# Turning the next group's rows between two projections, in the stage between two attentions

## The reference

```
x = x + _layernorm(_L1_attn_ref(...))            # end of the first attention
x = x + _layernorm(_L1_ffn_ref(_layernorm(x), ...))
# inside _L1_ffn_ref, e_cnt = 4, n = t // 4 tokens in each slice e:
for e in range(e_cnt):
    xn = _layernorm(x[:, e * n:(e + 1) * n, :], norm_w, norm_b)
    m = d // 2 ** e                              # 256, 128, 64, 32 features
    xm = xn[..., :m]
    qs.append(jnp.einsum('bnm,dm->bnd', xm, q_w[:, :m]) + q_b)
    ks_.append(jnp.einsum('bnm,dm->bnd', xm, k_w[:, :m]) + k_b)
    vs.append(jnp.einsum('bnm,dm->bnd', xm, v_w[:, :m]) + v_b)
```

## Time and profile before

| | us |
|---|---|
| median of 3 runs | 5305.97 |
| the 3 runs | 5304.77, 5305.97, 5321.23 |
| the profiled execution's own time | 5311.03 |
| its span (first to last instruction) | 5309.0 |
| mean granted TensorE clock in it | 0.927 of full |

### The profile page before, as it was taken

One profiled execution on the slowest core, in us unless ns is written; L12 is line 12 of the kernel. 1 busy time (PEld: TensorE's weight loads), 2 busy tenths in 40 slices (PEclk: granted clock), 3 DMA queues, 4 the chain that ended last, 5 costly groups with the idle time before them and its releaser, 6 DMA issues. The chain is left out here.

```text
span 5309.0 us, 99607 instructions
## 1 busy us (share of the span) xinstructions
PE 4817.8 (91%) x34169; PEld 2145.1 (40%) x34169; DVE 4244.5 (80%) x5541; ACT 3476.3 (65%) x6200; POOL 1333.0 (25%) x875
## 2 busy tenths in 40 slices
PE   6999677689699999999999999999998879999983
PEld 3444444156233333333333333333334445555532
DVE  6999650069699999999999999999994867777736
ACT  4777210123288888888888888888886316666663
POOL 2333210046200000000000000000000219999991
PEclk9999885689599999999999999999998659999996
DMA  5110567758633333333333333333321951323204
GB/s 179 52 52 36 175 226 269 258 174 276 132 47 47 52 57 47 47 51 50 56 47 47 47 54 55 47 47 55 53 33 48 309 145 41 73 64 78 67 5 161
DMA packets 345325, 499.06 MB, mean 94 GB/s; under 512 B 66688, under 2 KB 253856, under 8 KB 327808
## 3 DMA queue, kind: packets, MB, share of 16 engines
q1 hardware_dynamic: 332032, 475.86, 37.7%
q10 hardware_dynamic: 12800, 16.78, 0.9%
HBM read 325.15 MB, written 165.02 MB: 92 GB/s over the span
## 5 line engine op out<-in xcount | busy, mean ns | idle before, releaser
L771 DVE TENSOR_REDUCE at_NM<-at_MX 128x1 f32<-128x1024 f32 (+1 forms) x3008 | 3082.1, 1050 | 331.6 <-PE at_MX L603 300.1
L713 ACT ACTIVATE at_PB<-at_S 128x512 f32<-128x512 f32 x5056 | 2719.8, 597 | 605.1 <-PE at_S L632 498.3
L603 PE MATMUL at_MX<-at_KT,at_QT 48*128 48x512 f32 (+1 forms) x5056 | 1923.8, 456 | 74.2 <-DMA at_VS<-v 53.4
L632 PE MATMUL at_S<-at_QT,at_KT 50*128 50x512 f32 (+1 forms) x5056 | 1905.3, 442 | 6.1 <-ACT at_PB L713 5.8
L644 PE MATMUL at_AV<-at_PB,at_VS 128*32 128x256 f32 (+1 forms) x18304 | 1575.1, 415 | 15.3 <-ACT at_AVS L721 13.0
L632 PEld LDWEIGHTS at_S<-at_QT,at_KT 50*128 50x128 f32 (+1 forms) x5056 | 802.8, 187 | 883.0 <-issue 477.6
L603 PEld LDWEIGHTS at_MX<-at_KT,at_QT 48*128 48x128 f32 (+1 forms) x5056 | 792.8, 190 | 326.7 <-DVE at_NM L771 213.7
L644 PEld LDWEIGHTS at_AV<-at_PB,at_VS 128*32 128x32 f32 x18304 | 364.4, 108 | 863.3 <-ACT at_PB L713 743.1
L537 POOL CAST at_NMR<-at_NMF 16x128 fp32r<-16x128 f32 x79 | 22.1, 280 | 1638.5 <-ACT at_NMF L726 1638.5
L564 POOL TENSOR_TENSOR at_SUM<-at_SUM,at_PB 128x2048 f32<-128x2048 f32 x90 | 415.3, 4615 | 11.2 <-ACT at_PB L713 0.4
L911 PE MATMUL wkv_PQ<-wkv_XT,wkv_WT 128*128 128x512 f32 x768 | 340.3, 600 | 42.6 <-DVE wkv_DL L1031 25.9
(11 more groups left out here) (204 smaller groups left out, 3711.0 us busy)
## 6 DMA issues: line engine op xcount, KB each, us to landing
moe_W<-in_w SPq DMA_DIRECT2D x64, 1024.0 KB, 10.3
at_QT<-qk SPq DMA_DIRECT2D x408, 128.0 KB, 5.5
at_KT<-qk SPq DMA_DIRECT2D x384, 128.0 KB, 7.2
qk<-r_HI SPq DMA_DIRECT2D x52, 512.0 KB, 4.9
qk<-r_LO SPq DMA_DIRECT2D x52, 512.0 KB, 5.4
at_VS<-v SPq DMA_DIRECT2D x96, 256.0 KB, 8.9
at_KT<-qk SPq DMA_DIRECT2D x96, 256.0 KB, 6.3
ycat<-wkv_Y SPq DMA_DIRECT2D x32, 512.0 KB, 2.6
```

Of the source, the lines that this page charges most:

```text
L603: ins = nc.tensor.matmul(MX[r][:, a, :], q_of(s)[h:h + NQ, b * P:(b + 1) * P], k_of(it, s, b * P // W)[h:h + NQ, (c + a) * W:(c + a + 1) * W],
L632: nc.tensor.matmul(SP_[item(it, s, "score", t)[1]][:, :], k_of(it, s, c)[h:h + NQ + 2, kb * P:(kb + 1) * P], q_of(s)[h:h + NQ + 2, c * W:( ...
L713: nc.scalar.activation(PB[:, t % NPB, :], SP_[r][:, :], ACT.Exp, scale=scale).then_inc(exp_done, 1)
L771: nc.vector.tensor_reduce(NM4[:, b, c:c + 1], MX[r][:, :, :].rearrange("p a n -> p (a n)"), AX_X, ALU.max, negate=True).then_inc(ring_got, 1)
```

## The change

`project` is cut in two, and `turn` of the next group is put between the halves. `turn(0)` now stands ahead of the loop. No instruction is added or removed, and only PE's order changes.

```diff
-            def project(g):
+            def project_qk(g):
                 e, u = g % E4, g % 2
                 ks = rows(e)
                 wait(pe, xt, g + 1)
...
                     ins.then_inc(proj, 1)
+
+            def project_v(g):
+                u, ks = g % 2, rows(g % E4)
                 wait(pe, v_done, g)
                 for j in range(J):
...
                 ins.then_inc(vproj, 1)
 
+            turn(0)
             for g in range(NGR):
-                turn(g)
-                project(g)
+                project_qk(g)
+                if g + 1 < NGR:
+                    turn(g + 1)
+                project_v(g)
```

## The result

Over seven runs each, the changed kernel takes 5335.63 us (5330.24 to 5355.5) and the kernel before 5309.87 us (5304.77 to 5321.23). The ratio is 1.005, with a 95% interval of 1.0035 to 1.0065, so it is slower by 19 to 35 us. The forecast was 5335, from 5322 to 5346.

The account below looks back on a forecast made before the run. DVE was taken to bound plain passes, PE full-width ones. Eleven plain passes of 13.88 us, three full-width of 14.06 and the last put the stage 29.8 us later, 29.0 after the clock's credit: 5335 us, range 5322 to 5346.

Parts of the forecast that it names:

- The loop: Between PE and DVE: inner, turn, values of the group before, VB, next pass, inner; claimed to close, +23 to +39 us.
- Its price in a plain pass: Loop steps 8.40, 0.05, 1.78, 3.62 and 0.03 us: 13.88 us per plain pass, against 10.29 before.
- The clock in groups 1, 5, 9 and 13: Turn and values there form one 5.2 us slow-clock stream; an early rise credited 0.2 us each, 0.8 in all.
- My earliest row: Full-width stream from 4102.06: clock rose about 3.5 us after its start; such a rise would save 0.85 us.
- The full-width passes: Groups 4, 8, 12: PE goes on without waiting, 9.55 us projection, 0.86 turn, 3.62 values, 0.03: 14.06 us each.
- The first pass: VB(0): values start 0.86 us later, behind the turn, giving VB at 4115.30; nothing waits for inner(1).
- The sum: From VB(0) at 4115.30: 152.7 plain, 42.2 full-width, 8.9 last; VB(15) at 4319.1, 29.8 us later, +29.0 after the clock's credit.
- The marks I had set: VB waiting for PV in nearly all 16 groups, 40 us and more; turn waiting about 3 or 6 us; 13.9 us passes.
- A reading that was too simple: Kernel before: DVE sets the end of plain passes, 10.29 us each, and PE that of full-width ones.
- The rule about a busy TensorE: Skill's rule that a busy TensorE reaches full clock; by it the sum would be rival B's, 5299 us, chance 0.05.

Follow-up runs that it names:

- e5: Changed kernel, but DVE takes a group's values one pass later, just ahead of inner, and SP stores them later; ratio 0.9987 against the kernel before.
- e3: Changed kernel with the projections of the 64- and 32-row groups padded to 128 rows by zero weights; ratio 1.0036 against the kernel before.
- e4: Kernel before with the projections of the 64- and 32-row groups padded to 128 rows by zero weights; ratio 0.9975 against the kernel before.

## Why the prediction was right

**The loop.** It closes as written: inner, turn, values, VB. e5 shows that it is the cause, since moving the waiting end of it takes the whole loss away with PE's order as in the change.

**Its price in a plain pass.** Forecast 13.88 us, measured 14.18 to 14.19 in the passes of 64 and 32 rows. Between VB and the end of `inner` it is 8.41 us (forecast 8.40). The turn's spacing is 1.90, between the forecast 1.78 and its bound of 1.97. The values are 3.78 us behind a turn, where I took 3.62 from the rows behind queries and keys. These two are the 0.3 us.

**The clock in groups 1, 5, 9 and 13.** I took off 0.2 us each, from one early and one late rise. VB(1) came 13.08 us behind VB(0), and the other three passes are 12.8, 12.7 and 12.7, since the clock rose inside the values all four times. From the start of the values to that of the next stream are 2.33 to 2.75 us; at the slow clock throughout these are 3.41 (4131.22 to 4134.63 in e3's timeline). So the rise saved 0.7 to 1.1 us each time. In the last of them (values at 4281.81, next at 4284.14) it came 3.0 us after the turn's start at 4280.05: half of the slow time that was left, 2 x 1.08, was saved. My earliest row had it at 3.5. Of the term I expected 0.8 us in all and got 4.3, against my 13.88 a pass: this is the one that I mis-sized.

**The full-width passes.** Forecast 14.06, measured 13.8, 13.6 and 13.6; the projection takes 9.2 to 9.4 us from start to start (9.55).

**The first pass.** I had VB(0) later by the 0.86 us of the turn alone. It comes 14.53 us behind the first queries and keys, and came 12.38 behind them before, 2.2 us more. The projection took 10.0 us to the next start, against 8.7: the clock rose about 6.1 us after their start (0.50 until 4098, 0.95 in 4098 to 4103), where it was 3.5.

**The sum.** From VB(0) to VB(15): forecast 203.0 with the clock's credit, measured 4307.25 - 4106.89 = 200.4. With the first pass the stage is 27.7 us longer against a forecast of 29.0. The terms that erred nearly cancelled, which is luck too: the plain passes came out 2.1 us higher (7 of them at 0.3), the clock's term 3.5 lower, the full-width passes 1.2 lower and the first 1.3 higher. The time differs by 25.8 us from a median of 5309.87; mine was added to 5306.0, so part of the agreement at 5335 is luck: 3.9 us too low a start and 3.2 us too large a loss.

**The marks I had set.** VB waits in all 16 groups, 46.3 us (forecast 40 and more), 3.8 us in those of 64 and 32 rows (3.4). The turn waits 3.10 us behind the groups of 32 rows, as forecast, and 5.9 behind groups 1, 5, 9 and 13 (forecast 6). It waits 5.74 behind those of 64 rows, where I had 3.1: with the clock up inside the values, the queries and keys of 64 rows ran at the full clock (2.84 us). They were not on the path.

**A reading that was too simple.** I had DVE setting the end of all plain passes. In the kernel before, VB(7) and VB(11) wait for PV too, and their passes are 11.24 and 11.37 us, not 10.29:

```profile
4193.24 1.23 DVE L1607 TENSOR_TENSOR r_VB<-r_PV,r_BVE 128x1024 f32<-128x1024 f32 x1 [0.87 <-PE r_PV L1508]
...
4241.28 1.23 DVE L1607 TENSOR_TENSOR r_VB<-r_PV,r_BVE 128x1024 f32<-128x1024 f32 x1 [0.98 <-PE r_PV L1508]
```

The sum doesn't suffer, as it is set against the place of the last VB and not against 16 times a pass.

**The rule about a busy TensorE.** By the Trainium skill (TensorE: Matmul & The Clock Gate, section "Why this matters for your kernels") PE kept busy should have come to the full clock. The traces here don't agree with that where the operands are low. With the operands 128 rows high (e4) the same matmuls have a mean granted clock of 0.85, with 64 and 32 rows in half of the groups 0.69, although PE was busy in 135.12 of 179 us of e4's stage and in 164.24 of 190 before. Being busy was not enough in this kernel.

## What to carry to other kernels

Before work is moved ahead of an instruction, look at what the moved work waits for and who waits for what is now behind it. If both are the same engine, the move closes a loop, and its length is the sum of all its steps. Such a loop can be cut at its other end, by taking the waiting instruction a pass later; here that took the whole loss back.

A piece that runs faster helps only if it lies in the loop. In e3 the projection of queries and keys in the groups of 64 and 32 rows ran nearly twice as fast (2.86 us in place of 5.48) and the passes between VB(0) and VB(14) took as long as before (191.8 and 191.5 us), because behind the gap it left (5.85 us) the two pieces that counted ran at the slow clock (1.97 and 3.58 us).

## What the runs showed of the hardware that I had not expected

Weights of zero beyond row 64 or 32 made the kernel faster by 0.25%: the mean granted clock of the stage went from 0.69 to 0.85 with the same number of matmuls and columns, and PE's busy time from 164.24 to 135.12 us.

The values matmuls of 64 and 32 rows took 3.78 us for 8 instructions behind a turn and 3.62 behind the queries and keys, at the same clock of 0.50. Those of 128 rows took 3.62 and 3.58 behind a turn at that clock in e3. So a change of height between two streams seems to cost 0.16 us; this was seen in the rows and not tested by itself.
